# Layer-2 routed experts: weights, lists and gathers begun in the attention's last batch; added rows in four buffers

## Chip, cores and metric

One Trainium2 chip, one core. The time is device microseconds (us) of the whole kernel. The kernel before took 2472.98 us, the median of three runs (2466.5 to 2476.64).

## What is computed

The input is x, 16 batches of 256 tokens with 512 channels in float32. Two layers are added to it, each a mixer and a feed-forward with experts:

```
x = x + tanh(g_xattn[0]) * wkv(layernorm(x), ctx)
x = x + tanh(g_ffn[0])   * moe0(layernorm(x))        # 8 experts, top 2, and a shared one
x = x + tanh(g_xattn[1]) * causal_attention(layernorm(x), ctx, ctx)   # 16 heads of 32
x = x + tanh(g_ffn[1])   * moe1(layernorm(x))
# moe1: 64 experts, top 6, 352 hidden channels, at most 64 tokens for an expert, and
# a shared part of 704 hidden channels:
#   y[e] = (silu(buf[e] @ w_gate[e]) * (buf[e] @ w_up[e])) @ w_down[e]
#   out[t] = sum over the 6 experts of t of weight * y[e, slot] + shared(t)
```

Only the last layer's attention and `moe1` are touched here. `moe1` reads all 64 experts' weights from memory: 64 x 3 x 512 x 352 x 4 bytes, about 138 MB.

## The kernel before, in words

The kernel runs in phases, one behind the other: setup, wkv, routed experts of layer 1, `attention_phase` (L1080), `routed1_phase` (L1718). Each phase opens a `Memory` object. Its buffers, banks and semaphores live for the phase. On leaving it, the semaphores are cleared and all engines meet at a barrier (`Memory.__exit__`). Within a phase each engine has its own program, written out by hand, and engines wait for each other on semaphores with absolute counts. There is no planner.

*Attention.* A loop over the 16 batches, eight units (pairs of heads) each. Behind the attention of batch b run the shared feed-forward, the router's choice and the scatter of batch b - 1. For every choice the scatter writes a row (token number, weight) into `list1`, at the place that the expert's count gives (L1513, GpSimd, 12 indirect DMAs a batch). After the last batch, TensorE still has that batch's shared feed-forward to do alone. SP loads batch b + 1 while b is worked on, and stores two results: `xn1` (the normed rows that the experts will read, L1204) and `out` (the residual with the shared part, L1209). In the end it does `store_x3(LAST.before())`, `store_xn(LAST)`, `store_x3(LAST)` and waits until all four streams of stores have landed. GpSimd ends with a wait for all scatters. Buffers: two of each input, `stage` for loading the shared weights at the start only, `prT`, `at` and others.

*Routed experts of layer 2.* 64 experts are taken as 32 pairs (`PAIRS1`); the two experts of a pair lie in the two halves of 128 rows (64 places each). Weights have four slots (`SLOTS1`), lists eight. For pair q:

- SP (L1775 to L1793) loads the list of the pair, then gate and up weights (two DMAs of 1408 KB, once `up` of pair q - 4 is done), then down weights (two of 512 KB and two of 192 KB, once `y` of pair q - 4 is done).
- GpSimd (turn at L1819 to L1825) issues the gather of pair q + 3 (L1805), which needs its list and a free `xg`, and then the add of pair q - 2 (L1815): an indirect DMA that adds the 128 result rows to `out`. Each add waits until the add before it has landed, since two pairs can hold the same token.
- TensorE: transposes the gathered rows of q + 1 (L1844), then `gate` of q (L1850), `merge` of q - 2 (L1897), transposes of the hidden rows of q - 1 (L1869), `up` of q (L1850), `down` of q - 1 (`routed_y_ps`, L1880), the matrix of token numbers (`ids`, L1889).
- ScalarE copies the transposed rows (L1925), scales the result rows (L1930) and takes silu (L1939).
- VectorE: token numbers (L1958), `merged` of q - 2 into `ym` (L1982), `hT` of q - 1 (L1953), the product of silu and up (L1993), and `places` (L1968 to L1973): which rows of a pair name the same token (`same`), and where each row is added (`place`).

`ym` and `place` have two buffers each. So VectorE waits for the add of pair q - 2 before it writes them, in `places` (L1968) and in `merged` (L1982):

```
if third(q):
    two = q.before().before()
    dve.wait_ge(merged_s, q.i - 1)
    alone(dve)
    dve.wait_ge(added[two.s % SLOTS1], 16 * uses(two))
```

An engine's waits and instructions are in order: behind this wait stand, on VectorE, the next pair's token numbers, `merged` and `hT`, and TensorE's `down` waits for `hT`.

Of the kernel before, what the change touches and what calls it, by code (L numbers as in the profile page):

```python
# [14 lines left out]
P = 128  # L15
# [17 lines left out]
WAYS1, SLOTS1, AHEAD1 = 8, 4, 3  # L33
# [97 lines left out]
class Memory:  # L131
# [18 lines left out]
    def __exit__(self, *a):  # L150
        self.nc.clear_and_free_semaphores(self.sems)
        self.nc.all_engine_barrier()
        self.stack.close()

# [925 lines left out]
def attention_phase(nc, io, c):  # L1080
# [3 lines left out]
    with Memory(nc, "attn_") as m:  # L1084
        x = [m.sb(f"x_{s}", [P, TJ, C]) for s in range(2)]
        ctx = [m.sb(f"ctx_{s}", [P, TJ, C]) for s in range(2)]
        y0 = m.sb("y0", [P, K0, TJ, C])
        q_tok = m.sb("q_tok", [P, TJ, C])
        qT = [m.sb(f"qT_{s}", [P, KC, T]) for s in range(2)]
        kT = [m.sb(f"kT_{s}", [P, KC, T]) for s in range(2)]  # L1090
# [3 lines left out]
        prT = [m.sb(f"prT_{n}", [P, 2, 3, P]) for n in range(4)]  # L1094
        outT = [m.sb(f"outT_{n}", [P, T]) for n in range(2)]
        den, rden = m.sb("den", [P, TJ, HEADS]), m.sb("rden", [P, TJ, HEADS])
        at = m.sb("at", [P, TJ, HEADS, D])
# [10 lines left out]
        stage = [m.sb(f"stage_{n}", [P, 2 * S1]) for n in range(2)]  # L1108
# [44 lines left out]
        with nc.Block() as block:  # L1153
# [26 lines left out]
            def _(sp):  # L1180
# [41 lines left out]
                for n in range(PARTS):  # L1222
                    if n >= 2:
                        sp.wait_ge(high_s, n - 1)
                        sp.wait_ge(low_s, n - 1)
                    if n < KC:
                        for z, name in enumerate(("sw_gate", "sw_up")):
                            w = io[name][n * P:(n + 1) * P, :]
                            at0, at1 = z * WHOLE, 2 * WHOLE + z * (S1 - WHOLE)
                            sp.dma_start(stage[n % 2][:, at0:at0 + WHOLE], w[:, 0:WHOLE]).then_inc(staged[n % 2], 16)  # L1230
                            sp.dma_start(stage[n % 2][:, at1:at1 + S1 - WHOLE], w[:, WHOLE:]).then_inc(staged[n % 2], 16)
                    else:
                        k = n - KC
                        sp.dma_start(stage[n % 2][0:width(k), 0:C], io["sw_down"][k * P:k * P + width(k), :]).then_inc(staged[n % 2], 16)
                turns(sp, B, turn)
                store_x3(LAST.before())
                store_xn(LAST)
                store_x3(LAST)
# [256 lines left out]
            def _(pool):  # L1495
# [39 lines left out]
                for s in range(2):  # L1535
                    pool.wait_ge(scat[s], 16 * TJ * K1 * (B // 2))
# [181 lines left out]
def routed1_phase(nc, io, c):  # L1718
# [4 lines left out]
    with Memory(nc, "routed1_") as m:  # L1723
# [5 lines left out]
        wgu = [[m.sb(f"wgu_{s}_{z}", [P, 2, KC, H1]) for z in "ab"] for s in range(SLOTS1)]  # L1729
        wdn = [[m.sb(f"wdn_{s}_{z}", [P, HW, C]) for z in "ab"] for s in range(SLOTS1)]  # L1730
        pair = [m.sb(f"pair_{s}", [P, 2], I32) for s in range(WAYS1)]
# [3 lines left out]
        place = [m.sb(f"place_{s}", [P, 1], I32) for s in range(2)]  # L1735
        xg = [m.sb(f"xg_{s}", [P, C]) for s in range(SLOTS1)]
# [5 lines left out]
        ym = [m.sb(f"ym_{s}", [P, C]) for s in range(2)]  # L1742
# [4 lines left out]
        up_in = [m.sem(f"gate_up_in{s}") for s in range(SLOTS1)]  # L1747
        down_in = [m.sem(f"down_in{s}") for s in range(SLOTS1)]
        pair_in = [m.sem(f"pair_in{s}") for s in range(SLOTS1)]
        xg_in = [m.sem(f"rows_gathered{s}") for s in range(SLOTS1)]  # L1750
# [7 lines left out]
        with nc.Block() as block:  # L1758
            def of(name, e):

                return io[name][bass.ds(e, 1)].rearrange("a r n -> (a r) n")

# [10 lines left out]
            @block.sync  # L1773
            def _(sp):
                def turn(q):  # L1775
                    slot = q.s % SLOTS1
                    wait(sp, added[slot], 16 * (uses(q) - WAYS1 // SLOTS1))
                    alone(sp)
                    wait(sp, pair_in[slot], 16 * (uses(q) - 1))
                    alone(sp)  # L1780
                    sp.dma_start(pair[q.s][:], io["list1"][bass.ds(q.i * P, P), :]).then_inc(pair_in[slot], 16)  # L1781
# [3 lines left out]
                    for z in range(2):  # L1785
                        sp.dma_start(wgu[slot][z][:].rearrange("p z k n -> p (z k n)"), of("w_gu1", 2 * q.i + z)).then_inc(up_in[slot], 16)
# [3 lines left out]
                    for z in range(2):  # L1790
                        sp.dma_start(wdn[slot][z][:, 0:FULL, :].rearrange("p k n -> p (k n)"), of("w_down1", 2 * q.i + z)  # L1791
                                     ).then_inc(down_in[slot], 16)
                        sp.dma_start(wdn[slot][z][0:REST, FULL, :], of("w_down1_rest", 2 * q.i + z)).then_inc(down_in[slot], 16)  # L1793

                rounds(sp, PAIRS1, turn, WAYS1)

            @block.gpsimd
            def _(pool):
                def gather(q):
                    if later(q):  # L1800
                        pool.wait_ge(xt_s, q.i - SLOTS1 + 1)
                        alone(pool)
                    pool.wait_ge(pair_in[q.s % SLOTS1], 16 * uses(q))
                    alone(pool)
                    nc.gpsimd.indirect_dma_start(xg[q.s % SLOTS1][:], None, io["xn1"],  # L1805
                                                 bass.IndirectOffsetOnAxis(ap=pair[q.s][:, 0:1].bitcast(U32), axis=0)
                                                 ).then_inc(xg_in[q.s % SLOTS1], 16)

                def add(q):
                    pool.wait_ge(ym_s, q.i + 1)  # L1810
                    alone(pool)
                    if not q.first:
                        pool.wait_ge(added[q.before().s % SLOTS1], 16 * uses(q.before()))
                        alone(pool)
                    nc.gpsimd.indirect_dma_start(io["out"], bass.IndirectOffsetOnAxis(ap=place[q.s % 2][:].bitcast(U32), axis=0),  # L1815
                                                 ym[q.s % 2][:], None, compute_op=ALU.add).then_inc(added[q.s % SLOTS1], 16)
# [10 lines left out]
                ahead = first(PAIRS1, WAYS1)  # L1827
                for n in range(AHEAD1):
                    gather(ahead)
                    ahead = ahead.after()  # L1830
# [116 lines left out]
            def _(dve):  # L1947
# [12 lines left out]
                def places(q):  # L1960

                    dve.wait_ge(ids_s, q.i + 1)
                    if third(q):
                        two = q.before().before()
                        dve.wait_ge(merged_s, q.i - 1)
                        alone(dve)
                        dve.wait_ge(added[two.s % SLOTS1], 16 * uses(two))
# [5 lines left out]
                    v.scalar_tensor_tensor(place[q.s % 2][:], apart[:], twice[:], token[q.s % 2][:], ALU.mult, ALU.add).then_inc(place_c, 1)  # L1973

                def merged(q):
                    dve.wait_ge(merged_s, q.i + 1)
                    dve.wait_ge(place_c, 3 * q.i + 3)
                    if third(q):
                        two = q.before().before()
                        alone(dve)  # L1980
                        dve.wait_ge(added[two.s % SLOTS1], 16 * uses(two))
                    v.tensor_copy(ym[q.s % 2][:], merged_ps[:]).then_inc(ym_s, 1)  # L1982
# [20 lines left out]
                merged(last(PAIRS1, WAYS1))  # L2003

# [23 lines left out]
def build(nc, io):  # L2028
    with Memory(nc, "") as m:
# [6 lines left out]
        for phase in (attention_phase, routed1_phase):  # L2036
            phase(nc, io, c)
# [49 lines left out]
```

## Time and profile before

| | |
|---|---|
| median of the runs | 2472.98 us |
| profiled execution, its own time | 2463.79 us |
| its span in the trace | 2462.1 us |
| TensorE busy | 2079.0 us (84%) |
| VectorE busy | 1242.4 us (50%) |
| ScalarE busy | 737.1 us (30%) |
| GpSimd busy | 817.9 us (33%) |
| DMA over the span | 128 GB/s, 315.28 MB |
| first instruction of the routed stage of layer 2 | about 1978.9 us |

The shares are means over phases with different limits: the last fifth of the span, the routed stage, has another balance than the rest. A row of the trace names the line of the program, the engine, the tile written and the tiles read. PE is TensorE, PEld its weight loads, DVE is VectorE, ACT is ScalarE, POOL is GpSimd, SPq the DMA queue of SP. A DMA's time from issue to landing is not busy time of an engine. In a chain of waits every row is the work or transfer that the next row waited for. PEclk 1.00 is TensorE's full clock of 2.4 GHz, 0.50 is 1.2 GHz.

### The profile page before, as it was taken

The numbers are of one execution on the slowest core, as the hardware profiler recorded it, in microseconds if no ns is written. First come the engines' busy times: TensorE is split into PE (matmuls) and PEld (weight loads), VectorE is DVE, ScalarE is ACT, GpSimd is POOL, SyncE is SP. The second block draws the span as 40 slices with busy tenths as digits, with TensorE's granted clock in tenths as the row PEclk, the third lists the DMA queues.
The fourth block names the chain that finished last, engine by engine and source line by source line (L and its number), as shares of the span: only waits on it lengthen the run. The fifth ranks groups of instructions, "written<-read, shape, count | busy, mean of one in ns | idle before, by whom it ended". The sixth has DMA issues, their size and how long they took to land. (4 is left out here: it accounts for less than half of the span.)

```text
span 2462.1 us, 38884 instructions
## 1 busy us (share of the span) xinstructions
PE 2079.0 (84%) x11938; PEld 1408.1 (57%) x11939; DVE 1242.4 (50%) x2853; ACT 737.1 (30%) x2144; POOL 817.9 (33%) x822
## 2 busy tenths in 40 slices
PE   1899888894999999479999999999999846878786
PEld 1666666662555555257777777777777622333332
DVE  5777888863222222246676766666675501211221
ACT  2222222212222222244444444444444100111110
POOL 4455555531333333212333333433332401111211
PEclk9999999997999999659999999999999868888888
DMA  8232222213332232321111112211110089999994
GB/s 267 78 86 85 85 71 83 85 43 103 96 94 90 93 94 91 129 81 61 61 61 62 61 66 100 79 62 61 62 61 18 18 311 358 345 343 352 368 352 105
DMA packets 134409, 315.28 MB, mean 128 GB/s; under 512 B 37811, under 2 KB 46003, under 8 KB 126069
## 3 DMA queue, kind: packets, MB, share of 16 engines
q1 hardware_dynamic: 107380, 260.68, 30.5%
q0 software_dynamic: 26880, 52.68, 7.8%
q8 instruction: 88, 1.44, 0.3%
q14 instruction: 61, 0.49, 0.1%
HBM read 253.13 MB, written 62.33 MB: 128 GB/s over the span
## 5 line engine op out<-in xcount | busy, mean ns | idle before, releaser
L1422 ACT ACTIVATE attn_pr<-attn_score_ps,attn_nmax 128x128 f32<-128x128 f32 (+1 forms) x512 | 208.4, 419 | 194.7 <-DVE attn_nmax L1550 194.7
L948 PE MATMUL routed_gu_ps<-first_ffn_wgu,routed_xT 128*128 x576 | 261.2, 596 | 0.0
L1513 POOL DMA_INDIRECT list<-attn_pair,attn_pos x192 | 191.6, 998 | 74.4 <-issue 74.1
L310 PE MATMUL attn_ffn_ps<-attn_xnT_high,attn_wgu_high 128*128 128x256 f32 x704 | 210.1, 298 | 4.1 <-DVE attn_hT_low L1641 3.3
L310 PE MATMUL attn_ffn_ps<-attn_xnT_high,attn_wgu_low 128*128 128x256 f32 x704 | 201.5, 286 | 3.1 <-issue 3.1
L310 PE MATMUL attn_ffn_ps<-attn_xnT_low,attn_wgu_high 128*128 128x256 f32 x704 | 201.5, 286 | 1.4 <-issue 1.4
L1880 PE MATMUL routed_y_ps<-routed_wdn_a,routed_hT 128*64 128x512 f32 (+1 forms) x192 | 118.3, 766 | 81.8 <-DVE routed_hT L1953 81.8
L282 POOL TENSOR_SCALAR attn_norm_var_eps<-attn_norm_mean_var 128x2 f32<-128x2 f32 x32 | 7.9, 248 | 536.8 <-DVE attn_norm_mean_var L276 536.8
L948 PEld LDWEIGHTS routed_gu_ps<-first_ffn_wgu,routed_xT 128*128 128x128 f32 x576 | 104.9, 192 | 104.6 <-issue 104.6
L1550 DVE TENSOR_REDUCE attn_nmax<-attn_score_ps 128x2 f32<-128x256 f32 (+1 forms) x256 | 130.4, 551 | 63.0 <-PE attn_score_ps L1279 59.0
L1968 DVE TENSOR_SCALAR routed_same<-routed_ids_ps,routed_token 128x128 f32<-128x128 f32 x32 | 11.2, 351 | 297.4 <-DMA out<-routed_ym,routed_place 295.0
L911 POOL DMA_INDIRECT y<-routed_ys,routed_pair x72 | 73.5, 1021 | 248.2 <-DVE routed_ys L1063 241.8
L1555 DVE COPY attn_prT<-attn_tr_ps 128x384 f32<-128x384 f32 x128 | 70.8, 553 | 164.6 <-PE attn_tr_ps L1290 121.2
L1290 PE MATMUL attn_tr_ps<-ident,attn_pr 128*128 128x128 f32 x768 | 115.7, 289 | 41.9 <-ACT attn_pr L1422 39.3
L1805 POOL DMA_INDIRECT routed_xg<-xn,routed_pair x32 | 31.3, 979 | 356.2 <-DMA routed_pair<-list 334.7
L478 PE MATMUL wkv_ffn_ps<-wkv_xnT,wkv_wg 128*128 128x256 f32 x512 | 147.4, 439 | 0.0
L310 PEld LDWEIGHTS attn_ffn_ps<-attn_xnT_high,attn_wgu_high 128*128 128x128 f32 x704 | 137.2, 195 | 11.3 <-issue 6.9
L310 PEld LDWEIGHTS attn_ffn_ps<-attn_xnT_high,attn_wgu_low 128*128 128x128 f32 x704 | 137.0, 195 | 3.7 <-issue 3.7
L310 PEld LDWEIGHTS attn_ffn_ps<-attn_xnT_low,attn_wgu_high 128*128 128x128 f32 x704 | 137.3, 195 | 1.2 <-issue 1.2
L494 PE MATMUL wkv_ffn_ps<-wkv_wd,wkv_hT 128*128 128x512 f32 x256 | 114.1, 599 | 24.9 <-DVE wkv_hT L772 23.5
L1925 ACT COPY routed_xT<-routed_xt_ps 128x512 f32<-128x512 f32 x32 | 18.8, 586 | 366.3 <-PE routed_xt_ps L1844 338.8
L478 PE MATMUL wkv_ffn_ps<-wkv_xnT,wkv_wu 128*128 128x256 f32 x512 | 127.6, 394 | 0.0
(254 smaller groups left out, 5031.9 us busy)
## 6 DMA issues: line engine op xcount, KB each, us to landing
routed_wgu_a<-in_w_gu SPq DMA_DIRECT2D x32, 1408.0 KB
routed_wgu_b<-in_w_gu SPq DMA_DIRECT2D x32, 1408.0 KB
wkv_x<-in_x SPq DMA_DIRECT2D x32, 512.0 KB, 3.6
attn_y<-y SPq DMA_DIRECT2D x32, 512.0 KB
routed_wdn_a<-in_w_down SPq DMA_DIRECT2D x32, 512.0 KB
routed_wdn_b<-in_w_down SPq DMA_DIRECT2D x32, 512.0 KB
wkv_vT<-in_ctxT SPq DMA_DIRECT2D x16, 512.0 KB
xn<-wkv_xn SPq DMA_DIRECT2D x16, 512.0 KB
```

The lines of the kernel that those rows point to most:

```text
L310: ins = nc.tensor.matmul(out, a[i], b[j], start=start and n == 0, stop=stop and n == 2)
L478: ins = nc.tensor.matmul(ffn_ps[n % 2][:, col:col + T], w[:, k, n * P:(n + 1) * P], xnT[:, k, :], start=(k == 0), stop=(k == KC - 1))
L494: ins = nc.tensor.matmul(ffn_ps[j][:], hT[:, k, j * P:(j + 1) * P], wd[:, k, :], start=(k == 0), stop=(k == M0 - 1))
L911: nc.gpsimd.indirect_dma_start(io["y0"], bass.IndirectOffsetOnAxis(ap=pair[t.s][:, 1:2].bitcast(U32), axis=0), ys[t.s % SLOTS0][:], None, ...
L948: ins = nc.tensor.matmul(gu_ps[t.s % 2][:], xT[t.s % 2][:, k, :], wgu[:, bass.ds(e, 1), k, :].rearrange("p a n -> p (a n)"), start=(k == 0 ...
L1290: ins = nc.tensor.transpose(tr_ps[bank][:, col * P:(col + 1) * P], pr[u % 2][:, z // 3, z % 3, :], c.ident[:])
L1422: nc.scalar.activation(pr[u % 2][:, a, j:2 * j + 1, :].rearrange("p k t -> p (k t)"), score_ps[:, a, j * P:(2 * j + 1) * P], ACT.Exp, bias ...
L1513: nc.gpsimd.indirect_dma_start(io["list1"], bass.IndirectOffsetOnAxis(ap=pos[b.s][:, j, k:k + 1], axis=0), pair[b.s][:, j, k, :], None, bo ...
L1550: v.tensor_reduce(nmax[u % 2][:, :, j], score_ps[:, :, j * P:(2 * j + 1) * P], AX.X, ALU.max, negate=True).then_inc(max_s, 1)
L1555: v.tensor_copy(prT[u % 4][:, 0].rearrange("p k t -> p (k t)"), tr_ps[0][:, 0:3 * P]).then_inc(tr_ev[0], 1)
L1805: nc.gpsimd.indirect_dma_start(xg[q.s % SLOTS1][:], None, io["xn1"], bass.IndirectOffsetOnAxis(ap=pair[q.s][:, 0:1].bitcast(U32), axis=0)) ...
L1880: ins = nc.tensor.matmul(y_ps[half, :], hT[0:r, k, half], wdn[q.s % SLOTS1][z][0:r, k, :], start=(k == 0), stop=(k == HW - 1))
```

## The change

- A new class `Late` is made in a `Memory` of its own around the last two phases. It holds `room`, one buffer with space for the gate, up and down weights of two pairs (slots 0 and 1), the eight list buffers, the four buffers of gathered rows, and the semaphores of lists, gathers and weights.
- The attention puts `stage`, `y0`, `ctx`, `kT`, `qT`, `q_tok`, `x`, `at` and three of four `prT` into `room`, in that order: what is spent first lies in slot 0.
- SP, after its last turn of the attention: waits until the last batch's first scores are there, all merges done and the second last batch's values done, and issues the six weight DMAs of pair 0. After `store_x3(LAST.before())` it waits for the last scores, values, outputs and the residual, and issues those of pair 1. After `store_xn(LAST)` it waits for all scatters and issues the lists of pairs 0, 1 and 2 (`AHEAD1`), then `store_x3(LAST)`.
- GpSimd, after the last scatter, waits for the stores of `xn1` instead of the scatters, then for each of three lists, and issues the three gathers.
- In the routed stage SP leaves out the lists of pairs 0 to 2 and the weights of pairs 0 and 1 (`EARLY1` = 2), GpSimd the first three gathers.
- `ym` and `place` have four buffers, and VectorE waits for the add of pair q - 4.

```
-WAYS1, SLOTS1, AHEAD1 = 8, 4, 3
+WAYS1, SLOTS1, AHEAD1, EARLY1 = 8, 4, 3, 2
...
                 turns(sp, B, turn)
+                sp.wait_ge(score_s, UNITS * LAST.i + 1)
+                sp.wait_ge(merged, K0 * B)
+                sp.wait_ge(pv_s, GROUPS * LAST.i)
+                weights_ahead(0)
                 store_x3(LAST.before())
+                sp.wait_ge(score_s, UNITS * B)
+                sp.wait_ge(pv_s, GROUPS * B)
+                sp.wait_ge(out_ev, GROUPS * B)
+                sp.wait_ge(x3_s, B)
+                weights_ahead(1)
                 store_xn(LAST)
+                for s in range(2):
+                    sp.wait_ge(scat[s], 16 * TJ * K1 * (B // 2))
+                for s in range(AHEAD1):
+                    c.late.load_pair(sp, io, s, s)
                 store_x3(LAST)
...
                 for s in range(2):
-                    pool.wait_ge(scat[s], 16 * TJ * K1 * (B // 2))
+                    pool.wait_ge(xn_out[s], 16 * (B // 2))
+                for s in range(AHEAD1):
+                    pool.wait_ge(c.late.pair_in[s], 16)
+                    c.late.gather(nc, io, s)
...
+                    if not isinstance(q.i, int) or q.i >= AHEAD1:
...
+                    if not isinstance(q.i, int) or q.i >= EARLY1:
+                        c.late.load_up(sp, io, 2 * q.i, slot, wgu[slot])
...
+                    if not isinstance(q.i, int) or q.i >= EARLY1:
+                        c.late.load_down(sp, io, 2 * q.i, slot, wdn[slot])
...
                     if third(q):
-                        two = q.before().before()
                         dve.wait_ge(merged_s, q.i - 1)
                         alone(dve)
-                        dve.wait_ge(added[two.s % SLOTS1], 16 * uses(two))
+                    if later(q):
+                        dve.wait_ge(added[q.s % SLOTS1], 16 * (uses(q) - 1))
+                        alone(dve)
...
-                    v.tensor_copy(ym[q.s % 2][:], merged_ps[:]).then_inc(ym_s, 1)
+                    v.tensor_copy(ym[q.s % SLOTS1][:], merged_ps[:]).then_inc(ym_s, 1)
...
+class Late:
+    SLOT = 2 * (2 * KC * H1) + 2 * (-(-H1 // P) * C)
+    def __init__(self, m):
+        self.room = m.sb("room", [P, EARLY1 * self.SLOT])
+        self.pair = [m.sb(f"pair_{s}", [P, 2], I32) for s in range(WAYS1)]
+        self.xg = [m.sb(f"xg_{s}", [P, C]) for s in range(SLOTS1)]
...
-        for phase in (attention_phase, routed1_phase):
-            phase(nc, io, c)
+        with Memory(nc, "second_ffn_") as f:
+            c.late = Late(f)
+            for phase in (attention_phase, routed1_phase):
+                phase(nc, io, c)
```

## Rows read from the trace of the kernel before

**Rows 1.** The page, forty slices of the span: granted TensorE clock, DMA share, rate.
```profile
PEclk9999999997999999659999999999999868888888
DMA  8232222213332232321111112211110089999994
GB/s 267 78 86 85 85 71 83 85 43 103 96 94 90 93 94 91 129 81 61 61 61 62 61 66 100 79 62 61 62 61 18 18 311 358 345 343 352 368 352 105
```

**Rows 2.** Stages: length, busy us by engine, granted clock, DMA share, GB/s.
```profile
1800.00:1820.00 20.00, 19.25 (x129) 14.02 (x130) 12.90 (x27) 9.43 (x32) 8.46 (x10) 1.00 0.52 184
1980.00:2000.00 20.00, 1.08 (x4) 0.71 (x4) 0.15 (x1) 0.59 (x1) 1.96 (x2) 0.50 1.00 373
2007.70:2046.70 39.00, 30.83 (x161) 13.74 (x159) 5.21 (x16) 4.79 (x9) 2.85 (x4) 0.91 1.03 364
2060.00:2404.90 344.90, 280.90 (x1395) 117.52 (x1393) 66.15 (x200) 41.04 (x76) 63.94 (x50) 0.88 1.02 352
2456.00:2462.10 6.10, 0.00 (x0) 0.00 (x0) 0.00 (x0) 0.00 (x0) 0.00 (x0) 0.50 0.00 0
```

**Rows 3.** Waits from 1979 to 2462 us: total us, times, longest us.
```profile
POOL routed_xg L1805 <- DMA routed_pair<-list: 334.7, 30, 13.0
DVE routed_same L1968 <- DMA out<-routed_ym,routed_place: 295.0, 30, 19.1
```

**Rows 4.** The chain of waits, 2186 to 2217 us: start, us, what.
```profile
2188.00 9.25 DMA out<-routed_ym,routed_place
...
2198.97 0.56 DVE routed_hT L1953
...
2199.77 5.40 PE routed_y_ps L1880 x12
...
2207.74 5.88 DMA routed_pair<-list
...
2214.69 0.44 POOL routed_xg L1805
...
2215.98 8.58 DMA out<-routed_ym,routed_place
```

**Rows 5.** DMA issues from 1900 to 1980 us: count, KB, us to landing.
```profile
routed_pair<-list SPq DMA_DIRECT2D x1, 1.0 KB, 1.7
```

**Rows 6.** GpSimd's timeline, four gathers: start, us, what, idle before.
```profile
1995.43 0.97 POOL L1805 DMA_INDIRECT routed_xg<-xn,routed_pair  x1 [12.98 <-DMA routed_pair<-list]
...
2020.44 0.95 POOL L1805 DMA_INDIRECT routed_xg<-xn,routed_pair  x1 [11.82 <-DMA routed_pair<-list]
...
2046.66 0.95 POOL L1805 DMA_INDIRECT routed_xg<-xn,routed_pair  x1 [11.81 <-DMA routed_pair<-list]
...
2404.93 0.98 POOL L1805 DMA_INDIRECT routed_xg<-xn,routed_pair  x1 [11.29 <-DMA routed_pair<-list]
```

**Rows 7.** SP's DMA queue in time: three stores, the first weights.
```profile
1870.67 0.39 SPq L1204 DMA_DIRECT2D xn<-attn_xn  x1
...
1929.02 0.37 SPq L1209 DMA_DIRECT2D out<-attn_x  x1
...
1974.96 0.37 SPq L1209 DMA_DIRECT2D out<-attn_x  x1
...
1979.33 0.43 SPq L1786 DMA_DIRECT2D routed_wgu_a<-in_w_gu  x1
```

**Rows 8.** GpSimd's timeline, the last scatter of the attention.
```profile
1968.51 0.97 POOL L1513 DMA_INDIRECT list<-attn_pair,attn_pos  x1 [0.30 <-issue]
```

**Rows 9.** The gathered rows' tile, 2050 to 2400 us.
```profile
DMA to landing us min/median/max: 6.3/6.7/8.0
```

**Rows 10.** The chain of waits after 2420 us: start, us, what.
```profile
2421.99 0.44 PE routed_xt_ps L1844 x4
...
2431.84 2.52 PE routed_gate_ps L1850 x16
```

More of the change, by code:

```diff
@@ L1084, in attention_phase @@
     with Memory(nc, "attn_") as m:
[L1085 to L1090, printed above, removed]
+        room = c.late.place
+        stage = [room(2 * S1) for _ in range(2)]
+        y0 = room(K0, TJ, C)
+        ctx, kT, qT = [room(TJ, C)], [room(KC, T)], [room(KC, T)]
+        q_tok = room(TJ, C)
+        x = [room(TJ, C) for _ in range(2)]
+        ctx, kT, qT = ctx + [room(TJ, C)], kT + [room(KC, T)], qT + [room(KC, T)]
         nmax = [m.sb(f"nmax_{n}", [P, 2, TJ]) for n in range(2)]
         pr = [m.sb(f"pr_{n}", [P, 2, 3, P]) for n in range(2)]
-        prT = [m.sb(f"prT_{n}", [P, 2, 3, P]) for n in range(4)]
+        at = room(TJ, HEADS, D)
+        prT = [room(2, 3, P) for n in range(3)] + [m.sb("prT_3", [P, 2, 3, P])]
         outT = [m.sb(f"outT_{n}", [P, T]) for n in range(2)]
         den, rden = m.sb("den", [P, TJ, HEADS]), m.sb("rden", [P, TJ, HEADS])
-        at = m.sb("at", [P, TJ, HEADS, D])
         x3 = [m.sb(f"x3_{s}", [P, TJ, C]) for s in range(2)]
@@ L1734, in routed1_phase @@
         twice, spare, apart = m.sb("twice", [P, 1]), m.sb("spare", [P, 1]), m.sb("apart", [P, 1])
-        place = [m.sb(f"place_{s}", [P, 1], I32) for s in range(2)]
-        xg = [m.sb(f"xg_{s}", [P, C]) for s in range(SLOTS1)]
+        place = [m.sb(f"place_{s}", [P, 1], I32) for s in range(SLOTS1)]
         xT = [m.sb(f"xT_{s}", [P, KC, P]) for s in range(2)]
@@ L1741, in routed1_phase @@
         ys = m.sb("ys", [P, C])
-        ym = [m.sb(f"ym_{s}", [P, C]) for s in range(2)]
+        ym = [m.sb(f"ym_{s}", [P, C]) for s in range(SLOTS1)]
         xt_ps, ht_ps = m.ps("xt_ps"), m.ps("ht_ps")
@@ L1776, in turn @@
                     slot = q.s % SLOTS1
[L1777 to L1781, printed above, removed]
+                    if not isinstance(q.i, int) or q.i >= AHEAD1:
+                        wait(sp, added[slot], 16 * (uses(q) - WAYS1 // SLOTS1))
+                        alone(sp)
+                        wait(sp, pair_in[slot], 16 * (uses(q) - 1))
+                        alone(sp)
+                        c.late.load_pair(sp, io, q.i, q.s)
                     if later(q):
@@ L1804, in gather @@
                     alone(pool)
[L1805 to L1807 removed]
+                    c.late.gather(nc, io, q.s)
                 def add(q):
@@ L1814, in add @@
                         alone(pool)
-                    nc.gpsimd.indirect_dma_start(io["out"], bass.IndirectOffsetOnAxis(ap=place[q.s % 2][:].bitcast(U32), axis=0),
-                                                 ym[q.s % 2][:], None, compute_op=ALU.add).then_inc(added[q.s % SLOTS1], 16)
+                    nc.gpsimd.indirect_dma_start(io["out"], bass.IndirectOffsetOnAxis(ap=place[q.s % SLOTS1][:].bitcast(U32), axis=0),
+                                                 ym[q.s % SLOTS1][:], None, compute_op=ALU.add).then_inc(added[q.s % SLOTS1], 16)
                 def turn(q):
@@ L1825, in turn @@
                         add(q.before().before())
[L1827 to L1830, printed above, removed]
                 turns(pool, PAIRS1, turn, WAYS1)
@@ L1977, in merged @@
                     dve.wait_ge(place_c, 3 * q.i + 3)
-                    if third(q):
-                        two = q.before().before()
+                    if later(q):
                         alone(dve)
-                        dve.wait_ge(added[two.s % SLOTS1], 16 * uses(two))
-                    v.tensor_copy(ym[q.s % 2][:], merged_ps[:]).then_inc(ym_s, 1)
+                        dve.wait_ge(added[q.s % SLOTS1], 16 * (uses(q) - 1))
+                    v.tensor_copy(ym[q.s % SLOTS1][:], merged_ps[:]).then_inc(ym_s, 1)
                 def turn(q):
```

63 lines of the change are left out of this document (46 added, 17 removed).

## The prediction

> **What bounds the kernel now.** I read the page's 40 slices first [rows 1]. Slices 31 and 32 (1846 to 1970 us), the end of the attention, show 0 tenths of DMA and 18 GB/s. From slice 33 on the layer-2 routed experts run: 8 to 9 tenths of DMA and 311 to 368 GB/s for seven slices. The table of stages [rows 2] sharpens this: from 2060 to 2404.9 us the DMA share is 1.02 at 352 GB/s while TensorE is busy 280.90 of 344.90 us. So in this stage the weights of 32 expert pairs stream through full DMA engines, and TensorE has room.
>
> The waits say something else at first sight [rows 3]: VectorE waits 295.0 us in its `same` comparison (L1968) for the added rows, and GpSimd 334.7 us for lists. The chain of waits shows the loop behind it [rows 4]: the add of one pair (9.25 us) lets VectorE go on to its hT copy at 2198.97, this lets TensorE do `y` at 2199.77, this frees a weight buffer, SP then issues the rest of a pair and the next list (2207.74), and the list (5.88 us) lets GpSimd gather (2214.69) and add (2215.98). One turn of the loop is 2215.98 - 2188.00 = 27.98 us and carries two pairs. Is the loop the bound, or the DMA? The list tells: 1 KB lands in 1.7 us on empty queues [rows 5] and takes 5.88 us here, so weights stand ahead of it. The loop has some 4 us of queueing in it that would shrink if the DMA could go faster. And before the first add was issued the cadence was the same but for the add's bytes: lists 3 and 5 reached GpSimd at 2020.44 and 2046.66 [rows 6], 13.1 us a pair; between the lists 5 and 31 it is (2404.93 - 2046.66) / 26 = 13.8 us. I take the DMA as the bound, and the loop as something that only keeps the arithmetic two pairs behind the weights.
>
> **The change part by part.**
>
> *Weights of pairs 0 and 1 ahead.* The routed stage has 30 pairs to load in place of 32, and its first weight DMA still is issued at 1979.33 [rows 7]. From there the DMA is full as before: slots 2 and 3 are free, which is two pairs or about 26 us of transfers, and slot 0 is freed by TensorE's pair 0 long before that. So every later list arrives two pairs sooner. The adds begin two pairs sooner as well, so what drops out are two intervals without an add: 2046.66 - 2020.44 = **26.2 us** [rows 6]. From below: two intervals at the whole stage's pace with adds would be 27.6 us; from above: 373 GB/s were seen in 1980 to 2000 [rows 2] against 364 in 2007.7 to 2046.7, which would make them 25.6.
>
> *What these loads meet in the attention.* Pair 0's issue stands in SP's queue behind the xn store of 1870.67 [rows 7] and ahead of the x3 store of 1929.02; pair 1's stands behind that one and ahead of xn's last store, which so is issued some 3 us later (six issues) and lands behind 13 us of weights, at about 1945. Nobody reads it before the gathers at 1974. Each pair takes some 13 us; both stretches have empty DMA engines [rows 1]. TensorE beside a DMA load: at 1800 to 1820 it is busy 19.25 of 20 us with a DMA share of 0.52 [rows 2]. I take zero; the ends are 0 (nothing there waits for DMA) and +5 us (a fifth of the 26 us of loads).
>
> *Lists and gathers at the hand-over.* SP now waits for the scatters, whose last is issued at 1968.51 [rows 8] and done with about 2 us later, at 1971.5. Three list loads follow, the first landing 1.7 us on [rows 5], at about 1974; three gathers at about 1.3 us each on GpSimd end near 1978. SP's x3 store goes out at 1974.96 as before, since TensorE sets it, and the stage begins behind its landing, at 1978.9. So the hand-over costs nothing, with 1 us in reserve; if list and scatter are 2 us slower, it costs up to 3. What is queued behind GpSimd's new waits is only the barrier. In the routed stage TensorE then starts pair 0 about 1 us after the barrier and not at 1995.43 + 6.7 = 2002.1 (list 1, and a gather's landing) [rows 6, 9]. This by itself gives nothing while the DMA bounds: after pairs 0 and 1 TensorE waits for pair 2's and 3's weights.
>
> *Added rows in four buffers.* VectorE waits for the add of four pairs ago. That add is issued when list q+1 lands, i.e. when weights q have, and lands 9 to 10 us later; VectorE needs it after `up` of pair q, some 16 us after these weights. So the wait of 295 us goes. What is late next is the gather: TensorE takes the rows of q+1 before the gate of q, and list q+1 lands with the end of weights q. TensorE thus starts pair q about 8 us after its weights, not two pairs late. In the middle of the stage this is worth nothing (DMA bound), at the end it shortens the tail. Before: from the last gather's issue at 2404.93 [rows 6] to the end of the span, 57.2 us. After: landing 6.7 [rows 9], the turn of pair 30 at the stage's mean of 280.90 / 344.90 x 13.65 = 11.1 us [rows 2], and then from the gate of pair 31 to the end as now, 2462.1 - 2431.84 = 30.3 [rows 10]: 48.1 us. Gain **9.1 us**. Bounds: 0, if TensorE is as late as today (rival 1); 10.4, if pair 30's turn is the 9.85 us between 2421.99 and 2431.84.
>
> *One more nest of memory at the end* (clearing of semaphores, a barrier). The stretch behind the last DMA, from 2456 to 2462.1 [rows 2], holds two such exits and the end: I take 1 us, between 0 and 3. The moved tiles, the longer `place` and `ym` lists and the helper functions change no instruction.
>
> *Sum:* -26.2 - 9.1 + 1 = **-34.3 us**. The profiled execution took 2463.8 us (span 2462.1) and would become 2429.5. It lies 9 us under the median of the runs shown (2473); the saving is the same there: **2439 us**.
>
> A page of the Trainium skill, "DMA: Bandwidth & Descriptors" (Specifications), puts HBM at about 358 GB/s per core. The rows have 352 in the steady stage and 373 over 20 us, so the ceiling is near but isn't strict. By 358 in place of 352 the sum would hardly move.
>
> **The rivals.**
>
> 1. *The loop, not the DMA, was the pace, and a loop through the adds stays* (GpSimd still issues a gather ahead of each add, and each add waits for the one before). Then the stage lasts 32 pairs at 13.8 as before and gains only TensorE's earlier start, 2002.1 - 1980.5 = 21.6, less the 1 us: 2473 - 20.6 = 2452. For it: 295 us in the waits. Against: the DMA share of 1.02 and the list's 5.88 us. Chance 0.12.
> 2. *The loop did hold the DMA back a little.* In 2007.7 to 2046.7, with deep queues, it moved 364 GB/s, later 352 [rows 2]. If this were the loop's doing, 3% of the remaining 28 pairs (385 us) or 12 us come on top: 2427. Against: the add costs more time per byte than a load, which explains it too. Chance 0.15.
> 3. *Slower: TensorE falls to the lower clock and becomes the bound.* Now it rests once in two pairs; then it would rest some 2.5 us in every pair. The granted clock is 0.50 while it stands in 1980 to 2000, 0.88 on average later [rows 2], so rests cost it clock. A turn at full clock is 9.85 us [rows 10] against 13.65 of DMA. It decides from 3.8 us of work a turn that runs at 1.2 instead of 2.4 GHz (7.6 us at the lower clock); with the whole turn at 1.2 GHz a pair takes 19.7 us and the stage is 32 x (19.7 - 13.65) = 194 us longer than the weights need, some 2630 us in all. Just 1.1 us a turn beyond 3.8 eats the 34. Against: in 2007.7 to 2046.7 TensorE already ran in just this rhythm, one rest a pair, with a clock of 0.91. Chance 0.03.
> The skill's "TensorE: Matmul & The Clock Gate" (HAM oscillation) tells of a kernel whose every burst starts at half clock because each is followed by a wait for DMA, which is this rival's mechanism; by that rule each turn would start slow, and the same window says that it would still fit.
> 4. *The early loads don't help,* because they disturb the attention or the hand-over by more than 5 us: contention, or SP held at a wait. 2445 to 2465. Nothing in the profile asks for it. Chance 0.07.
>
> **How the numbers follow.** The forecast has 0.60 (2431 to 2447 by its own terms and the spread of the runs, 2466.5 to 2476.6), the rivals 0.12, 0.15, 0.03 and 0.07, and 0.03 is for what I don't see. The range of 2425 to 2454 takes in rivals 1 and 2. Half a per cent, 12 us, is what a measurement can tell: faster than 2460.6 hold the forecast, rivals 1 and 2 and most of 4, 0.92; the same 0.04, slower 0.04.
>
> **What would show it.** Right: 30 pairs' weights behind 1979 and DMA share 1.0 with 345 to 365 GB/s to about 2389; a gather of list 31 near 2379; VectorE's wait for added rows gone, TensorE's long waits now for gathered rows and about 2 to 3 us in each pair; two humps of 13 us in the DMA row between 1870 and 1945; the start of the stage within 1 us of 1979; 48 us from the last gather to the end. Wrong: a DMA share clearly under 1 in the middle of the stage (then TensorE or a loop bounds), lists still reaching GpSimd at 13.8 us steps that begin only at 1995, or an attention that ends later than 1979 by more than 3 us.

## The result, and the profile after

The changed kernel takes 2443.41 us, the median of five runs (2439.51 to 2455.87), against 2469.7 (2460.59 to 2476.64) for the kernel before on the same chip. The ratio is 0.9918, with a 95% interval of 0.9891 to 0.9945: some 20 us faster by the ratio, 26 by the medians. 2439 was forecast, from a saving of 34. That the time lies only 4 us above the forecast is in part luck: the forecast started from 2473 of three runs, and with five runs the kernel before has 2469.7. The executions of one kernel lie some 16 us apart here, so two single profiles mislead: the profiled execution of the changed kernel was its slowest (2455.87, span 2454.1), only 8 us under the profiled one of before. What follows compares stretches, and sets several executions side by side.

The page of the changed kernel (granted clock, DMA share, rate in forty slices), which answers to [rows 1]:

```profile
PEclk9999999997999999659999999999999978888888
DMA  8232222212332233321111111122112269999994
GB/s 268 78 86 86 74 80 85 81 48 99 95 91 91 92 95 94 117 99 61 61 62 62 61 62 61 64 99 82 62 61 89 89 211 353 356 346 343 336 337 119
```

The two humps are there: 89 GB/s in slices 31 and 32 where 18 stood. They lie in time (SP's DMA queue; start, us, what), to be set beside [rows 7]:

```profile
1878.07 0.42 SPq L1209 DMA_DIRECT2D xn<-attn_xn  x1
1878.59 1.95 SPq L2057 DMA_DIRECT2D second_ffn_room<-in_w_gu  x2
...
1935.53 0.40 SPq L1214 DMA_DIRECT2D out<-attn_x  x1
1936.10 1.08 SPq L2057 DMA_DIRECT2D second_ffn_room<-in_w_gu  x2
...
1939.42 0.43 SPq L1209 DMA_DIRECT2D xn<-attn_xn  x1
...
1977.39 1.28 SPq L2066 DMA_DIRECT2D second_ffn_pair<-list  x3
1983.10 0.39 SPq L1214 DMA_DIRECT2D out<-attn_x  x1
1991.85 0.33 SPq L2057 DMA_DIRECT2D routed_wgu_a<-in_w_gu  x1
```

Pair 0 goes out right behind the xn store, pair 1 behind the x3 store of the second last batch, and xn's last store 3.4 us late, all as written. But from the last x3 store (1983.10) to the first weights of the stage (1991.85) it takes 8.75 us, where it was 4.4. The arrivals at GpSimd, beside [rows 6] (the gathers of lists 3, 5 and 31):

```profile
2007.73 0.95 POOL L2069 DMA_INDIRECT second_ffn_xg<-xn,second_ffn_pair  x1 [24.31 <-DMA second_ffn_pair<-list]
...
2033.98 0.95 POOL L2069 DMA_INDIRECT second_ffn_xg<-xn,second_ffn_pair  x1 [12.07 <-DMA second_ffn_pair<-list]
...
2405.82 0.98 POOL L2069 DMA_INDIRECT second_ffn_xg<-xn,second_ffn_pair  x1 [11.52 <-DMA out<-routed_ym,routed_place]
```

From the stage's first weights list 3 now takes 2007.73 - 1991.85 = 15.9 us, where it took 41.1: **25.2 us** saved. From the last gather's issue to the end of the span it is 2454.1 - 2405.82 = 48.3 us, where it was 57.2. But lists 5 to 31 come (2405.82 - 2033.98) / 26 = 14.3 us apart, not 13.8. The waits of the stage (total us, times, longest), beside [rows 3]:

```profile
DVE routed_same L1981 <- PE routed_ids_ps L1901: 80.4, 31, 3.0
PE routed_xt_ps L1856 <- DMA second_ffn_xg<-xn,second_ffn_pair: 76.9, 29, 4.9
```

VectorE's 295 us for added rows are gone: `same` (now L1981) waits at most 3.0 us, for TensorE. TensorE waits for gathered rows, 29 times. The stage as a whole and the stretches of the early weights (columns as in [rows 2]):

```profile
1870.00:1900.00 30.00, 25.47 (x178) 20.51 (x178) 10.43 (x23) 10.63 (x38) 13.14 (x16) 0.89 0.51 180
1930.00:1950.00 20.00, 18.35 (x93) 16.49 (x93) 6.46 (x21) 3.40 (x8) 13.14 (x16) 0.74 0.69 242
...
2034.00:2405.80 371.80, 298.93 (x1417) 128.18 (x1413) 69.19 (x206) 42.18 (x77) 66.43 (x52) 0.86 1.03 345
2448.00:2454.10 6.10, 0.00 (x0) 0.00 (x0) 0.00 (x0) 0.00 (x0) 0.00 (x0) 0.50 0.00 0
```

While pair 0 is loaded, TensorE is busy 25.47 of 30 us. The steady part moves 345 GB/s at a share of 1.03, and after the last add 6.1 us without DMA remain, as before.

### The profile page after: what moved, and what is told of

It is laid out like the page before. It is cut to its first block and busy times, and to the rows that moved or that the text cites. A ratio compares the mean times of both kernels' runs of the same rounds, so it can differ in the third digit from the quotient of the medians.

```text
span 2454.1 us, 38929 instructions
## 1 busy us (share of the span) xinstructions
PE 2100.9 (86%) x11938; PEld 1424.1 (58%) x11939; DVE 1243.5 (51%) x2853; ACT 737.3 (30%) x2144; POOL 817.3 (33%) x822
## 5 line engine op out<-in xcount | busy, mean ns | idle before, releaser
L2069 POOL DMA_INDIRECT second_ffn_xg<-xn,second_ffn_pair x32 | 31.3, 978 | 350.5 <-DMA second_ffn_pair<-list 222.7
L1580 DVE COPY second_ffn_room<-attn_tr_ps 128x384 f32<-128x384 f32 x96 | 52.9, 551 | 158.4 <-PE attn_tr_ps L1312 80.8
L1994 DVE COPY routed_ym<-routed_merged_ps 128x512 f32<-128x512 f32 x32 | 22.1, 691 | 214.9 <-PE routed_merged_ps L1909 214.9
L1058 DVE TENSOR_TENSOR routed_h<-routed_silu_gate,routed_gu_ps 128x256 f32<-128x256 f32 x72 | 30.3, 421 | 191.9 <-ACT routed_silu_gate L1017 191.9
L1301 PE MATMUL attn_score_ps<-second_ffn_room 32*128 32x128 f32 (+1 forms) x1024 | 126.0, 366 | 0.0
```

The lines of the kernel that those rows point to most:

```text
L1301: ins = nc.tensor.matmul(score_ps[:, a, j * P:(2 * j + 1) * P], qT[b.s][r:r + D, k, j * P:(j + 1) * P], kT[b.s][r:r + D, k, 0:(j + 1) * P] ...
L1580: v.tensor_copy(prT[u % 4][:, 0].rearrange("p k t -> p (k t)"), tr_ps[0][:, 0:3 * P]).then_inc(tr_ev[0], 1)
```

## The experiments

All times are medians; ratios are against the kernel before on the same chip, with 95% intervals. The first number of a row of stages is its window; each was cut from the gather of list 5 to that of list 31, so its length divided by 26 is the pace of a pair.

**The changed kernel again** (no edit).

> The changed kernel unchanged, for a second profile, since the first was 12 us above the median of its own runs. Theory D (behind TensorE that keeps close to the weights, the queue of loads is deeper, and the added rows land late and the DMA moves less): lists 5 to 31 again 14.3 us apart, adds landing in about 12 us, 335 to 345 GB/s late in the stage. Rival N (it was that execution): 13.8 us apart and 352 GB/s as before. Theory H (the gathers ahead hold up the hand-over): from the last x3 store's issue to the first weights of the stage again 8.7 us (before 4.4). Time 2443 either way.

2446.62 us, ratio 0.9904 (0.9875 to 0.9933). One row of stages, the landing of the adds (2080 to 2380 us) and the chain of waits:

```profile
2027.97:2386.57 358.60, 297.75 (x1417) 127.35 (x1415) 69.18 (x206) 42.11 (x77) 66.39 (x52) 0.87 1.03 357
```

```profile
DMA to landing us min/median/max: 8.3/11.1/12.6
```

```profile
2302.83 9.01 DMA second_ffn_xg<-xn,second_ffn_pair
...
2312.71 2.52 PE routed_gate_ps L1862 x16
...
2319.12 2.60 PE routed_y_ps L1892 x12
...
2325.14 19.03 DMA second_ffn_pair<-list
...
2344.94 8.82 DMA second_ffn_xg<-xn,second_ffn_pair
```

The pace is 13.8 us here, so the 0.5 us a pair of the first profile was in good part that execution: rival N. But the adds again take 11.1 us to land (7.2 before, over the same window), which is theory D's first half. The chain shows the new loop: a list of 1 KB stands 19.0 us behind weights, the gather takes 9.0, then TensorE does a turn and frees a buffer. Queueing is the longest part of the loop: the DMA bounds. The hand-over took 8.28 us. The time, 2443 expected, came out 3.6 us higher.

**Gathers in the stage.** GpSimd's loop moves from the end of the attention to the start of the routed stage.

```
-                for s in range(AHEAD1):
-                    pool.wait_ge(c.late.pair_in[s], 16)
-                    c.late.gather(nc, io, s)
...
+                for s in range(AHEAD1):
+                    pool.wait_ge(c.late.pair_in[s], 16)
+                    c.late.gather(nc, io, s)
                 turns(pool, PAIRS1, turn, WAYS1)
```

> As the changed kernel, but the three gathers are issued by GpSimd at the start of the routed stage; lists and weights still ahead. Theory H: the three gathers (768 KB) share the engines with the last x3 store, so that store and the barrier come late; here the stage starts 4.4 us after the store's issue again, and the time is 4 to 5 us less, about 2438.5, since TensorE has the slack to start 8 us later. Rival (the hand-over is long for another reason, such as the outer memory or the wait for lists): start still 8.7 us after the store, 2443 or up to 8 more for the later gathers.

2443.4 us, ratio 0.9887 (0.9858 to 0.9917), 3.2 us under the median of the changed kernel in the same job. SP's DMA queue:

```profile
1980.82 0.40 SPq L1214 DMA_DIRECT2D out<-attn_x  x1
1984.83 0.33 SPq L2057 DMA_DIRECT2D routed_wgu_a<-in_w_gu  x1
```

4.01 us from the store to the stage's first issue, as before the change (3.95 to its first list, 4.4 to its first weights). So the early gathers do lengthen the hand-over. The time moved the way that theory H says, by 3.2 us of the 4 to 5 expected, and the intervals overlap; 2438.5, the time expected, was missed by 5.

SP's waits at the end of the attention (total us, times, longest) and the DRAINs of GpSimd and SP (POOLq, SPq: ns, start in us; GpSimd's starts are rough), first in the changed kernel:

```profile
SPq L1263 <- DMA out<-attn_x: 4.6, 1, 4.6
...
SPq L1158 <- PEq L1158: 2.6, 1, 2.6
...
L1158 POOLq DRAIN  x1: 10203/10203/10203, 1980.7 to 1980.7; - x1
...
L1158 SPq DRAIN  x1: 7/7/7, 1988.4 to 1988.4; - x1
```

and here:

```profile
SPq L1263 <- DMA out<-attn_x: 2.3, 1, 2.3
...
SPq L1158 <- PEq L1158: 0.2, 1, 0.2
...
L1158 POOLq DRAIN  x1: 16262/16262/16262, 1966.0 to 1966.0; - x1
...
L1158 SPq DRAIN  x1: 7/7/7, 1983.8 to 1983.8; - x1
```

The x3 store does land 2.3 us later beside the gathers (4.6 for 2.3). But then SP stands another 2.6 us at the meeting: GpSimd's DRAIN ends at 1980.7 + 10.2 = 1990.9, 2.5 us behind SP's, and releases everybody. Here it ends at 1982.3, ahead of SP's. In all twelve profiles GpSimd's DRAIN ends 7.9 to 9.3 us after the issue of its last indirect DMA. In the five with early gathers that is 2.4 to 4.3 us behind SP; in the others it is never behind (1977.8 for SP's 1977.9 in the kernel before). So the early gathers set the start of the stage by when the last of them is issued. This is read from the traces; no run changes the DRAIN alone.

The gain is smaller than the hand-over's 4 us, since the gathers' bytes are back in the stream: list 3 here arrives 2002.94 - 1984.83 = 18.1 us after the first weights, not 15.9. From the x3 store's issue to list 3 it is 22.1 us here, 24.6 and 24.1 in the two profiles of the changed kernel.

**Two buffers.** Weights, lists and gathers ahead as in the change, added rows as before it.

```
+                        two = q.before().before()
...
-                    if later(q):
-                        dve.wait_ge(added[q.s % SLOTS1], 16 * (uses(q) - 1))
-                        alone(dve)
+                        dve.wait_ge(added[two.s % SLOTS1], 16 * uses(two))
...
-                    v.tensor_copy(ym[q.s % SLOTS1][:], merged_ps[:])
+                    v.tensor_copy(ym[q.s % 2][:], merged_ps[:])
```

> As the changed kernel, but added rows and places in two buffers, with the wait for the add of two pairs ago. My reckoning: the 9.1 us of the tail go back, 48 to 57 us from the last gather to the end, time 2452; under theory D the adds land in 7 us again and the lists come at 13.8 us, which gives up to 10 us back, so 2443 to 2452. Rival L (the loop through the adds was the pace, and the four buffers opened it): lists still 13.8 apart and the time 2452 or above, with the early weights worth under 15 us of 26.

2451.12 us, ratio 0.9913 (0.9885 to 0.9941). The stages, and the landing of the adds:

```profile
2033.21:2389.80 356.59, 281.45 (x1403) 117.64 (x1399) 68.27 (x208) 40.93 (x75) 66.41 (x52) 0.88 1.03 354
```

```profile
DMA to landing us min/median/max: 6.1/7.8/9.4
```

Pace 13.72, adds landing in 7.8 us, 57.7 us from the last gather (2389.80) to the end of the span (2447.5). So what was moved ahead pays 22 us without the four buffers, where rival L gave it under 15: L falls, although the time is within 1 us of L's 2452. The tail's 9 us went back, and the adds came early again. Against the changed kernel in the same job (2446.62) the four buffers are worth 4.5 us.

**Four buffers only**, in the kernel before. The edit is the change's in `places`, `merged`, `place` and `ym`.

> The kernel before with four buffers of added rows and places and the wait for the add of four pairs ago, nothing moved ahead. My reckoning: 9 us less than before by the tail alone, 2461; with theory D, 26 intervals at 14.3 in place of 13.8 take it back, 2461 to 2474. Rival L: the stage itself gets faster, under 13.6 us a pair and 2455 or less.

2467.54 us, ratio 0.9981 (0.9961 to 1.0): 5 us, with an interval from 0 to 10. The stages:

```profile
2048.52:2413.38 364.86, 300.74 (x1429) 129.84 (x1424) 69.48 (x208) 42.56 (x78) 66.40 (x52) 0.86 1.03 352
```

The last gather is at 2413.38 and the span 2462.8, so the tail is 49.4 us: the 8 us are there. The pace is 14.03, which takes back 6.5. Rival L falls here too: opened, the loop made nothing faster.

**Shallow**: fewer loads in SP's queue.

```
-                        sp.wait_ge(up_s, q.i - SLOTS1 + 1)
+                        sp.wait_ge(up_s, q.i - SLOTS1 + 2)
...
-                        sp.wait_ge(y_s, q.i - SLOTS1 + 1)
+                        sp.wait_ge(y_s, q.i - SLOTS1 + 2)
```

> The changed kernel, but SP issues the weights of pair q only when up and y of pair q - 3 are done (not q - 4), so that fewer loads stand in the queue when an add is issued. Four executions with four buffers so far: adds land in 11.1 to 12.3 us and lists come 13.8 to 14.3 us apart, with two buffers 7.2 to 7.8 us and 13.7 to 13.8. Theory D1 (the depth of SP's queue is what delays adds and gathers and costs the 0.25 us a pair): adds back at about 7 to 8 us, gathers at 6.7, lists 13.75 apart, time 5 to 7 us less than the changed kernel, about 2439. Rival D2 (it is not the depth but where in the stream of weights the add falls, or TensorE's rhythm): adds still near 12 us, 14.0 apart, 2444 to 2450; if the queue runs dry, over 14.2 apart and slower than that.

2447.22 us, ratio 0.9909 (0.9888 to 0.9929). Stages and landing:

```profile
2029.74:2388.93 359.19, 294.65 (x1438) 127.06 (x1436) 70.73 (x209) 42.64 (x78) 66.48 (x52) 0.89 1.02 353
```

```profile
DMA to landing us min/median/max: 6.2/6.3/9.4
```

The adds land in 6.3 us, half of 12, which is D1's first half: how far SP may run ahead changes it. A list of 1 KB, which stands behind the loads, takes 5.6 us (median, same window), 18.1 in the second profile of the changed kernel and 9.9 before the change. D1's second half, the time, was missed: 2439 expected, 2447 measured, no different from the changed kernel. The pace of 13.81 suggests a gain, but its hand-over took 10.3 us (GpSimd's DRAIN ended 4.3 us behind SP's), and one execution with four buffers and a deep queue had 13.79.

**Lists early.** Gathers in the stage, and each list two pairs ahead of its weights.

```
-                    if not isinstance(q.i, int) or q.i >= AHEAD1:
...
+                    l = q.after().after()
+                    if not isinstance(l.i, int) or AHEAD1 <= l.i < PAIRS1:
...
-                        c.late.load_pair(sp, io, q.i, q.s)
+                        c.late.load_pair(sp, io, l.i, l.s)
...
-                rounds(sp, PAIRS1, turn, WAYS1)
+                turns(sp, PAIRS1, turn, WAYS1)
```

> Gathers issued in the stage, and in the stage each list loaded ahead of the weights two pairs before its own. My reckoning that TensorE starts a pair late because the gather of the next rows can only begin when these weights have landed: it then starts with the weights, 7 to 9 us earlier; from the last weights to the end it is shorter by that, and with the hand-over's 4 us saved the time is about 2433. Since gathers are no longer at the list's landing, the adds are issued when their rows are ready. Rival: the stage's end is set by the last weights and adds only, or TensorE at the lower clock fills the slack: 2440 or more.

2437.21 us, ratio 0.9859 (0.9838 to 0.9881), between the 2433 expected and the rival's 2440. The stages:

```profile
2001.04:2375.02 373.98, 307.91 (x1509) 136.50 (x1510) 74.21 (x223) 45.32 (x83) 66.46 (x52) 0.88 1.03 344
```

List 31 now arrives ahead of the weights of pair 29, and from its gather (2375.02) to the end it is 69.4 us; in the changed kernel the same point lies two pairs before the list's landing, 48.3 + 2 x 14.0 = 76.3 us from the end. So TensorE does finish 7 us nearer to the weights. But the pace is 14.38, and part of it is lost there.

**Lists early, again.**

> The same kernel as lists_early, to see whether its 2437 holds against the changed kernel's 2443 to 2447. If the 8 us are real: 2435 to 2440 again, and the hand-over 4 to 5 us. If they were chance: 2443 or more.

2443.06 us, ratio 0.988 (0.9855 to 0.9905); hand-over 4.9 us, pace 14.1. The 8 us were not all real: the expected 2435 to 2440 was missed by 3, and 2443 is what the text gave for chance. The two ratios, 0.9859 and 0.988, against 0.9918 and 0.9904 of the changed kernel say 2 to 6 tenths of a per cent, and of the four comparisons only 0.9859 against 0.9918 has intervals that do not overlap. Against the gathers in the stage alone (0.9887) the early lists are not shown to gain.

**Lists early and shallow**, both edits.

> Both: lists two pairs ahead, gathers in the stage, weights of pair q after y of pair q - 3. Under D1 the adds land in 7 to 8 us and the time is 5 to 7 us under that of the lists early alone, about 2427; under D2 equal to it; TensorE starts earlier here, so the queue should not run dry.

2437.36 us, ratio 0.9863 (0.9834 to 0.9893), pace 13.94, adds in 8.8 us. Adds land earlier than in 12 us, but the time is that of lists early alone, and not the 2427 expected: the second half of D1 missed again. And a list takes 19.8 us here (median, 2080 to 2380 us), as long as with the deep queue. So a queue that is long by this measure went with adds that land in 8.8 us, and its depth alone does not account for the landing.

**No adds.** The adds of the routed rows are left out.

```
-                    nc.gpsimd.indirect_dma_start(io["out"], bass.IndirectOffsetOnAxis(ap=place[q.s % SLOTS1][:].bitcast(U32), axis=0),
-                                                 ym[q.s % SLOTS1][:], None, compute_op=ALU.add).then_inc(added[q.s % SLOTS1], 16)
+                    nc.gpsimd.engine_nop().then_inc(added[q.s % SLOTS1], 16)
```

> The changed kernel with the adds of the routed rows to the output left out (the output lacks the routed experts); all waits stay. It prices an add in the stream: 13.1 us was one pair without adds in the kernel before. If the add costs its ordinary share, lists are 13.1 apart here (0.7 us an add with two buffers, 0.9 with four), 24 us less in all, about 2419. If the slower pace with four buffers has nothing to do with adds, 13.35 or more.

2419.41 us, ratio 0.9795 (0.9759 to 0.9831). The stages:

```profile
2031.68:2377.58 345.90, 290.61 (x1425) 124.46 (x1425) 70.40 (x208) 42.17 (x77) 24.63 (x27) 0.90 1.03 349
```

Pace 13.30. Three executions with four buffers, adds and the deep queue of the changed kernel gave 14.30, 13.79 and 13.97 (mean 14.02), so an add costs 0.72 us a pair in the stream, about the 0.7 of the kernel before; 13.1 was not reached. The time is 24 and 27 us under the changed kernel's two medians, of which the adds in the stream make 19 and the shorter tail (40.6 for 48.7) some 8. So the expected time, 2419, was met with luck: the sum behind it had put all 24 us into the stream, and none into the tail.

**Weights only**: two buffers, lists and gathers in the stage. From the ends of SP's and GpSimd's programs in the attention:

```
-                for s in range(AHEAD1):
-                    c.late.load_pair(sp, io, s, s)
...
-                for s in range(AHEAD1):
-                    pool.wait_ge(c.late.pair_in[s], 16)
-                    c.late.gather(nc, io, s)
```

> Only the weights of pairs 0 and 1 are begun in the attention; lists and gathers in the routed stage as before, added rows in two buffers. If the parts add up as I now hold (two pairs off the stream 25 us, hand-over 4.4 us behind the last x3 store without gathers in front of it, tail of 57 us, adds landing in 7 to 8 us, lists 13.75 apart), it takes 24 to 26 us less than before, about 2445, so within 3 us of the whole change. Rival: the early weights need the early lists or the four buffers to pay, then 2452 or more.

2449.52 us, ratio 0.9915 (0.9893 to 0.9937). Stages:

```profile
2028.11:2388.23 360.12, 283.65 (x1403) 118.11 (x1400) 68.41 (x208) 40.99 (x75) 66.48 (x52) 0.87 1.02 351
```

20 to 21 us, from the first of the three parts alone. Pace 13.85, tail 57.8 us. It missed 2445 by 4.5, and the rival's 2452 by less; the ratio stands where that of the whole change stands. The profile accounts for it: list 3 arrives 2001.81 - 1984.03 = 17.8 us after the first weights, where it was 41.1, which is 23.3 us saved and not 25.2, since the three gathers are in the stream again. The hand-over takes back 1 us (the issue of three lists ahead of the weights), the pace 2 and the tail 0.6. That leaves 20.

Side by side, one profile each. The hand-over is from the last x3 store's issue to the stage's first weights, the tail from the gather of list 31 to the end of the span, the landing the median from 2080 to 2380 us. The stage's first issue, which is a list in some kernels, comes 3.95 to 4.01 us after the store in all seven without early gathers:

| kernel | ratio | hand-over | pace | adds land in | tail |
|---|---|---|---|---|---|
| before | 1 | 4.4 | 13.78 | 7.2 | 57.2 |
| weights only | 0.9915 | 5.4 | 13.85 | 7.3 | 57.8 |
| two buffers | 0.9913 | 8.2 | 13.72 | 7.8 | 57.7 |
| four buffers only | 0.9981 | 4.4 | 14.03 | 12.1 | 49.4 |
| changed | 0.9918 | 8.75 | 14.30 | 12.3 | 48.3 |
| changed, again | 0.9904 | 8.3 | 13.79 | 11.1 | 48.7 |
| gathers in the stage | 0.9887 | 4.0 | 13.97 | 11.9 | 49.2 |
| shallow | 0.9909 | 10.3 | 13.81 | 6.3 | 49.0 |
| lists early | 0.9859 | 4.9 | 14.38 | 12.2 | - |
| lists early, again | 0.988 | 4.9 | 14.10 | 11.6 | - |
| lists early, shallow | 0.9863 | 4.9 | 13.94 | 8.8 | - |
| no adds | 0.9795 | 8.3 | 13.30 | - | 40.6 |

## Why the prediction was right, and where it was off

The direction, the bound and the range held; the saving forecast, 34 us, was a third (against 26) to two thirds (against 20) too large.

- *Weights ahead, -26.2*: held as a sum, 25.2 us between the stage's first weights and list 3, and 25.3 in the second profile. But these two whole intervals hold gathers too. The weights alone took off 23.3 (weights only); the other 2 us are the early gathers' bytes, of which the prediction had said that they give nothing by themselves.
- *What the loads meet in the attention, 0 (to +5)*: held within what can be seen. The second last batch's `norm` to the last's, across pair 0's loads, took 60.7 and 61.3 us in the two kernels without them and 59.8 to 62.0 in the ten profiles with. From that `norm` to the last x3 store it was 50.6 and 53.1 without, 51.0 to 54.6 with: 1 us at most in the means.
- *Hand-over, 0 (to +3)*: **this step failed.** It counted the issue of the three gathers, which end near 1978, called what is queued behind GpSimd's waits "only the barrier", and took the x3 store's landing for the end of the phase. It left out GpSimd's DRAIN, which ends 8.1 to 8.6 us after the last gather's issue, 2.4 to 4.3 us behind SP's. With the gathers the hand-over is 8.2 to 10.3 us, without them 4.0 to 5.4: 4 us or more. The store beside the gathers' 768 KB landed some 2 us late as well, but was not the last to end. Against the 2 us that the gathers take out of the stream, having them ahead costs some 2 us net.
- *Four buffers, -9.1 at the tail and nothing in the middle*: the tail held to 0.2 us (48.3 for 48.1). The middle is **the term that was mis-sized**: "worth nothing (DMA bound)" took the queue's state as given. With TensorE close behind the weights the buffers come free sooner, a list stands 18.1 us in SP's queue in place of 9.9, adds land in 11 to 12 us in place of 7 to 8 and gathers in 7.5 to 8.9 in place of 6.7. The paces of the kernels with two buffers are 13.72, 13.78 and 13.85, those with four and the same depth 13.79, 13.97, 14.03 and 14.30: 0.24 us a pair on average, 6 us over 26 pairs. In time the four buffers gave 5 us (four buffers only) and 4.5 (against two buffers), half of the 9.1, though the interval of the first still holds 9. That adds land late because SP may run four pairs ahead is shown (shallow), with the depth of the queue as the likely reason but not the whole one (lists early and shallow). That this costs the pace is only suggested by single profiles whose ranges overlap, and no timed comparison with a shallower queue bore it out: the cause of the mis-sizing stays open.
- *One more nest, +1*: nothing seen, 6.1 us without DMA at the end in both.

Sum of what was found: -25.2 - 8.7 + 4 + 6 = -24, between the 20 of the ratio and the 26 of the medians. The 6 is a mean over single profiles, in which the first profile alone shows 13.6 and the second 0.3.

The rivals: the first (the loop was the pace) fell with two buffers and four buffers only. The second (deeper queues move more) is not seen: from 2080 to 2380 us the kernels with four buffers and adds move 341 to 356 GB/s, the kernel before 352. The fourth (early loads disturb by more than 5 us) came in part, as the 4 us of the hand-over. The third had its mechanism but not its price: after a wait for rows some turns start at the lower clock, the gate in 4.89 us where others take 2.52 (the chain of waits of the changed kernel, and the same two stretches with the columns of [rows 2]):

```profile
2196.58 2.52 PE routed_gate_ps L1862 x16
...
2284.89 4.89 PE routed_gate_ps L1862 x16
```

```profile
2196.58:2199.10 2.52, 2.52 (x18) 1.06 (x17) 0.00 (x0) 1.18 (x2) 0.00 (x0) 1.00 1.06 349
...
2284.89:2289.78 4.89, 4.89 (x17) 1.72 (x17) 0.00 (x0) 1.18 (x2) 0.75 (x1) 0.50 1.05 387
```

The granted clock is 1.00 (2.4 GHz) in the first, where TensorE had waited 1.4 us for the rows, and 0.50 (1.2 GHz) in the second, where it had waited 3.2. But the granted clock is 0.86 in the steady part (0.88 before), and a turn still fits in the pair's time, as it did in the window that the prediction named. The Trainium skill ("TensorE: Matmul & The Clock Gate", HAM oscillation) tells of a kernel in which every burst behind a wait for DMA starts at the lower clock. These rows agree as to the mechanism, but here only some of the turns do.

Lowest of the kernels that keep the adds are those with lists early and the gathers in the stage: 0.9859 and 0.988, and 0.9863 with the shallow queue. The gathers in the stage alone have 0.9887, which the intervals do not tell from them.

## What to carry to other kernels

In a stage that only streams from memory, bytes moved into an idle stretch ahead of it come off its length one for one, and making the compute follow sooner pays only in the tail. An indirect DMA that GpSimd issues "for free" just ahead of the end of a phase is not free: here the phase could end only 8 us after its issue, whoever else was done. Look at the end of every engine's program, not only at the last store, and issue such a transfer behind the barrier if nobody needs it yet. And with runs 16 to 20 us apart, read a change from the same stretches of several executions, not from two spans.

## What was not expected of the hardware

GpSimd's DRAIN at the end of the attention ends 7.9 to 9.3 us after the issue of its last indirect DMA, in all twelve profiles, with scatters of small rows as with gathers of 256 KB. What it waits for is not shown: in the changed kernel the DMA engines move nothing from 1988 to 1992.

The landing time of an indirect DMA from GpSimd depends on how far SP may run ahead with its loads, though these are in another queue: adds of 256 KB land in 6.3 us when SP may run three pairs ahead of `y` and in 11 to 12 when it may run four; with the lists early the same two settings give 8.8 and 11.6 to 12.2 (medians from 2080 to 2380 us). The Trainium skill ("DMA: Bandwidth & Descriptors", Queues, rings and completion order) says that an engine goes round its queues packet by packet. By that alone a queue that is never empty would delay the add by the same whatever its depth, which these medians do not bear out. The same section says that the write which raises the semaphore lands only after every earlier write of that engine, across its queues, which would let it depend on what else is under way; no run here separates this from other causes.
